# An attention and expert layer: another front, zeros on TensorE, and down weights and rotation table in other pieces

## The chip, the cores and the metric

One Trainium2 chip, one core of it, with its engines TensorE (PE; PEld is its weight load), VectorE (DVE), ScalarE (ACT), GpSimd (POOL) and SyncE (SP, here only an issuer of DMAs). Times are device microseconds of one execution of the whole program. All data are fp32 in DRAM.

## The reference

```python
x = hidden                                # [2048, 256], one batch
xn = layernorm(x)                         # no gain, eps 1e-5
q, k, v = xn @ W.T + b, 16 heads of 16    # q and k rotated (RoPE, even and odd channels)
scores = q k^T / 4; columns 205..1535 masked out   # 205 first and 512 last keys stay
attn = softmax(scores) @ v @ Wo.T + bo
expert = argmax(xn @ router_w.T)          # 8 experts, top 1 with top-2 softmax weight
ffn = weight * (silu(xn gate_w^T) * (xn up_w^T)) @ down_w^T    # inner width 176
out = x + attn + ffn
```

## The kernel before

The kernel is written engine by engine, each with its own program order; semaphores join them. There is no planner: the order around the change is written out by hand, and an engine that waits holds everything behind it on that engine.

**Front.** The 2048 tokens are 16 tiles of 128, in four groups g of four tiles, and eight pairs of two. SP loads x (the first two tiles, the other two of group 0, then groups 1 to 3; between groups 1 and 2 the constants `const`: identity, triangle, ones and some rows, and the router weights `rt`), then `wqk` (k and q weights in one DMA, lines 324 and 325 with the biases `bqk` on the same semaphore), `wv`, the broadcast biases `bvo` and the rotation table `tab` in one DMA of 2 MB (cosine and sine, 2048 columns each). Per group DVE makes statistics (`moments`, lines 903 to 908: four `bn_stats`, four `bn_aggr`, one addition of EPS), ACT the square root (`root`, 1293), DVE the reciprocal and the shift (913, 915), and DVE and ACT normalise two tiles each (919 and 1305; DVE all four in group 3). DVE does `moments(g)` before `normalize(g - 1)`. PE turns the tiles pair by pair (`turn_pair`, 570: four transposes of 128x128 into a PSUM bank), ACT copies a pair to `xnT` (1298), DVE the last pair (942).

**PE's order in the front** (lines 599 to 644): pairs 0 and 1; `project(0)` (594: keys of the first 205 tokens, two halves of 128 channels, two matmuls each); pairs 2 and 3; the router's logits of token block b=0 (576: each block b writes its own 32 rows of one bank); pairs 4 to 7; one of six chunks of v (583); the logits of blocks 1 to 3; one more v chunk; four transposes of the logits (624); two v chunks; the ranks (629 to 632); `project(1)`; two v chunks; 16 matmuls that sum tokens into slots (641), one for each of DVE's 16 lane tiles (1040); `project(2)` and `project(3)`. DVE meanwhile rotates `project(0)`, chooses experts and gives every token a row in an order sorted by expert (977 to 1062), writes the gather indices `token_of`, and then adds bv to the six v chunks into `v_all` (1092). POOL first fills rows of `k_op` and all of `v_all` with ones (481, 489), then waits for `token_of` and gathers the tiles of sorted rows (496), 23 of them. SP stores xn to DRAM group by group (341) for these gathers, loads gate/up weights (342, 2.8 MB), stores the first key part, and loads the down weights `dn` (344 and 345: rows 0 to 79 and 80 to 87 of 88, each row 16 KB; an expert's 176 inner rows are two halves of 88), waits for gather 1 and loads `wo`.

**Expert rows.** 23 steps: PE turns the gathered rows (653), gate and up (667), the hidden rows turned (692, twice 88 columns), down (680, twice 88 rows), and from step 7 maxima of the scores of heads 0 and 1 ahead of time (705), which DVE reduces (1116). The remaining projections and rotations are spread over the steps.

**Heads.** 16 heads of score matmuls (818), exponentials on ACT (1420), probabilities times v (789) and the next heads' maxima (716, 729; DVE 1122, 1125). POOL adds bo to the residual x tile by tile during the heads.

## Time and profile before

| | us |
|---|---|
| median of 3 runs (lowest, highest) | 379.26 (378.15, 379.45) |
| profiled execution, its own time | 379.26 |
| its span in the profile | 377.4 |
| PE busy | 360.1 |
| DVE busy | 331.2 |
| ACT busy | 265.4 |
| POOL busy | 70.1 |

The span is the time between the first and the last instruction seen by the profiler; 1.9 us lie around it. Matmuls are pipelined and their ends modelled, so the sums of PE overlap a little. A timeline row merges neighbouring instructions of one line: start, length, engine, line, operation, tiles, count, and in brackets how long the engine was idle before and what released it.

### The profile page before, as it was taken

To read this page: it belongs to the slowest core of one execution; us is meant where nothing else is said; L and a number is where in the kernel's file an instruction comes from. 1 tells how busy PE (TensorE), PEld (TensorE's weight loads), DVE (VectorE), ACT (ScalarE), POOL (GpSimd) and SP (SyncE) were. 2 spreads that over 40 slices of the span, in tenths; PEclk is the share of its full clock that TensorE was granted. 3 is DMA by queue.
4 is the path that set the end of the run, shared out by engine and by line. 5 is a ranking of instruction groups with operands and counts; after the bars stand their busy time and mean duration, and the time that the engine had idled before them with its cause. 6 is when DMAs were issued, how large, how long until landed. Compare 5 with 4: busy or idle time off the path is not lost.

```text
span 377.4 us, 12257 instructions
## 1 busy us (share of the span) xinstructions
PE 360.1 (95%) x4670; PEld 204.1 (54%) x4670; DVE 331.2 (88%) x684; ACT 265.4 (70%) x538; POOL 70.1 (19%) x87
## 2 busy tenths in 40 slices
PE   0899999999999999999999999999999999999994
PEld 0665566776664564555556546555455554543373
DVE  5869789998768999999999999999999999998464
ACT  1634577664446888888888888888888888899900
POOL 5002845333000021020220202123112021010020
PEclk9999999999999999999999999999999999999999
DMA  7999656756410212223132231322313212111116
GB/s 230 407 396 251 144 156 188 233 159 187 118 64 31 61 33 60 72 64 75 31 88 68 56 75 32 95 80 48 88 40 91 61 49 74 34 46 32 32 32 221
DMA packets 30795, 40.59 MB, mean 108 GB/s; under 512 B 10772, under 2 KB 25876, under 8 KB 30160
## 3 DMA queue, kind: packets, MB, share of 16 engines
q1 hardware_dynamic: 28680, 34.62, 30.9%
q0 software_dynamic: 1872, 5.11, 5.7%
q8 instruction: 38, 0.62, 0.7%
q10 hardware_dynamic: 192, 0.13, 0.1%
q14 instruction: 13, 0.11, 0.1%
HBM read 25.78 MB, written 11.70 MB: 99 GB/s over the span
## 4 chain that ended last, share of the span: by engine, by line
PE 92%; DMA 2%; ACT 2%; SPq 1%; DVE 1%; issue 1%; ACTq 0%; DVEq 0%
PE ps L789 22%; PE ps L818 21%; PE ps L716 14%; PE ps L667 7%; PE ps L729 6%; PE ps L594 5%; PE ps L680 5%; PE ps L797 3%; DMA bqk<-bqk_in 2%; PE ps L705 2%; PE ps L583 1%; PE ps L653 1%; PE ps L692 1%; PE ps L576 1%; PE ps L570 1%
## 5 line engine op out<-in xcount | busy, mean ns | idle before, releaser
L1122 DVE TENSOR_REDUCE mx<-ps 128x1 f32<-128x512 f32 x232 | 150.2, 683 | 4.3 <-PE ps L716 1.5
L1420 ACT ACTIVATE probs<-ps 128x512 f32<-128x512 f32 x192 | 101.9, 598 | 18.3 <-PE ps L818 17.3
L818 PE MATMUL ps<-q_op,k_op 98*32 98x512 bf16 (+1 forms) x1104 | 112.2, 381 | 0.1
L716 PE MATMUL ps<-k_op,q_op 96*32 96x512 bf16 x672 | 76.0, 381 | 0.0
L1125 DVE TENSOR_REDUCE mx_tail<-ps 128x2 f32<-128x410 f32 x116 | 66.8, 576 | 3.2 <-PE ps L729 3.1
L818 PEld LDWEIGHTS ps<-q_op,k_op 98*32 98x32 bf16 (+1 forms) x1104 | 39.6, 96 | 33.6 <-issue 5.6
L789 PE MATMUL ps<-probs,v_op 128*32 128x512 f32 x384 | 52.5, 592 | 0.0
L502 POOL COPY v_op<-v_all 128x192 f32<-128x192 f32 x16 | 7.0, 444 | 187.5 <-PE ps L789 187.5
L1420 ACT ACTIVATE dn<-ps 77x512 f32<-77x512 f32 x64 | 34.3, 592 | 8.2 <-PE ps L818 8.2
L496 POOL DMA_INDIRECT o_st<-sorted_rows,token_of x23 | 26.3, 1143 | 58.1 <-PE ps L653 28.5
L716 PEld LDWEIGHTS ps<-k_op,q_op 96*32 96x32 bf16 x672 | 25.1, 96 | 21.6 <-DVE mx L1122 9.0
L1420 ACT ACTIVATE gu<-ps 128x512 f32<-128x512 f32 x64 | 33.2, 604 | 5.0 <-PE ps L818 5.0
L818 PE MATMUL ps<-parts 98*32 98x512 bf16 (+1 forms) x368 | 36.3, 381 | 0.1
L729 PE MATMUL ps<-k_op,q_op 96*32 96x205 bf16 x672 | 35.7, 251 | 0.0
L729 PEld LDWEIGHTS ps<-k_op,q_op 96*32 96x32 bf16 x672 | 22.1, 97 | 23.1 <-issue 9.4
L1420 ACT ACTIVATE wqk<-ps 128x512 f32<-128x512 f32 x64 | 33.1, 608 | 0.1
L667 PE MATMUL ps<-gu,probs 128*128 x92 | 31.0, 459 | 0.0
L716 PE MATMUL ps<-parts 96*32 96x512 bf16 x256 | 28.4, 380 | 0.0
L1116 DVE TENSOR_REDUCE mx<-ps 128x1 f32<-128x717 f32 x24 | 21.7, 903 | 6.8 <-PE ps L705 6.1
L594 PE MATMUL ps<-xnT,wqk 128*128 128x512 f32 (+1 forms) x48 | 21.1, 584 | 0.2 <-DMA bqk<-bqk_in 0.2
L818 PEld LDWEIGHTS ps<-parts 98*32 98x32 bf16 (+1 forms) x368 | 12.7, 95 | 15.0 <-ACT probs L1420 4.5
L789 PE MATMUL ps<-dn,v_op 77*32 77x512 f32 x128 | 18.8, 592 | 0.0
(142 smaller groups left out, 489.3 us busy)
## 6 DMA issues: line engine op xcount, KB each, us to landing
q_parts<-parts SPq DMA_DIRECT2D x12, 256.0 KB, 2.8
sorted_results<-ys SPq DMA_DIRECT2D x23, 128.0 KB, 2.1
gu<-gu_in SPq DMA_DIRECT2D x1, 2816.0 KB, 14.2
q_op<-q_parts SPq DMA_DIRECT2D x11, 192.0 KB, 3.5
tab<-tab_in SPq DMA_DIRECT2D x1, 2048.0 KB, 11.5
sorted_rows<-xn SPq DMA_DIRECT2D x4, 512.0 KB, 6.3
xnT<-o_st SPq DMA_DIRECT2D x62, 32.0 KB, 2.3
tab<-softmax_recips SPq DMA_DIRECT2D x15, 128.0 KB
```

The source lines that it names most:

```text
L496: pool.indirect_dma_start(out=xs[t % XR], out_offset=None, in_=xn_dram, in_offset=bass.IndirectOffsetOnAxis(ap=token_of[:, t:t + 1], axis= ...
L594: ins = pe.matmul(proj_bank(u, odd), wqk[:, is_q, HID * m + P * odd:HID * m + P * odd + P], xnT[:, m, t0:t0 + n], start=m == 0, stop=m == ...
L667: ins = pe.matmul(bank(b)[:, 0:2 * I], xsT[b][:, P * m:P * m + P], gu[:, bass.ds(e * (HC * 2 * I) + 2 * I * m, 2 * I)], start=m == 0, stop ...
L680: ins = pe.matmul(bank(4 + b)[:, 0:HID], hidT[b][:, P * m:P * m + P], dn[:, bass.ds(e * (2 * HID) + HID * m, HID)], start=m == 0, stop=m == 1)
L716: ins = pe.matmul(bank(t % 2)[r:r + CW, :], q_op[slot][0:KR, P * t + r:P * t + r + CW], k_op[slot][0:KR, 0:NWIDE], start=True, stop=True)
L729: ins = pe.matmul(bank(2)[r:r + CW, NTAIL * n:NTAIL * n + NTAIL], q_op[slot][0:KR, P * t + r:P * t + r + CW], k_op[slot][0:KR, NWIDE:NK], ...
L789: ins = pe.matmul(bank(7)[VW * b:VW * b + VW, :], v_op[slot][0:rows, VW * c:VW * c + VW], prob[c][0:rows, QB * b:QB * b + QB], start=c == ...
L818: ins = pe.matmul(bank(4 + u % RING)[r:r + w, :], k_op[h % OPS][:, c0 + r:c0 + r + w], q_op[h % OPS][:, QB * b:QB * b + QB], start=True, s ...
L1116: dve.tensor_reduce(mx[:, h, t:t + 1], ps[:, EARLY_MAX:EARLY_MAX + NK], AX.X, ALU.max).then_inc(max_reduced, 1)
L1122: dve.tensor_reduce(mx[:, slot, t:t + 1], bank(t % 2)[:, 0:NWIDE], AX.X, ALU.max).then_inc(wide_reduced, 1)
L1125: dve.tensor_reduce(mx_tail[:, slot, 2 * pair:2 * pair + 2], bank(2)[:, 0:2 * NTAIL].rearrange("p (t n) -> p t n", t=2), AX.X, ALU.max).th ...
L1420: act.activation(prob[c][0:rows, QB * b:QB * b + QB], bank(4 + u % RING)[0:rows, :], ACT.Exp, scale=SCALE).then_inc(exp_done, 1)
```

## The change

- **x and constants.** The four groups of x are loaded without anything between them. The identity comes alone, on ACT's queue, as ACT's first instruction; triangle, ones and the rest come later on SP. Key weights, `bqk`, `rt`, `wv`, then the constants, the bias bo (broadcast) and bv as two columns, table part 0 and the query weights follow, each with a semaphore of its own.
- **Statistics.** `normalize(g)` follows `moments(g)` directly, with two of group 3's statistics in front of `normalize(2)`. EPS is the bias of ACT's square root, and the addition on DVE is gone. ACT normalises two tiles of group 3 as well and copies the last pair; DVE copies pair 6.
- **Zeros.** DVE clears 512 columns of `q_op[1]` first, and PE multiplies them into a bank that nothing reads yet: 16 times at the start, then 6, 2, 2 and 2 times between its groups of transposes.
- **PE's order.** Pairs 0 and 1, 2 and 3, `project(0)`, pairs 4 and 5, two v chunks, pairs 6 and 7, all four logits blocks side by side, a v chunk, the transposes of the logits, two v chunks, ranks, `project(1)`, the last v chunk, half of `project(2)`, the slot sums, the other half.
- **v bias.** v is copied without bias by ACT (six copies in place of DVE's six additions). Since the probabilities of a row sum to one, bv times Wo is added to bo: PE makes it with two matmuls ahead of head 0 (from `wo` and the bv columns), DVE adds it to the broadcast bo.
- **POOL.** `v_all` is filled first, the rows of `k_op` only after the logits.
- **Down weights.** The 176 rows of an expert are split as 128 and 48, not as 88 and 88. Three DMAs bring them in pieces of 1 KB: 88 rows, 40 rows (partitions 88 to 127) and 48 rows. They stand behind gate/up and table part 1 and no longer wait for the first key part.
- **Table.** Four DMAs of 512 columns: part 0 in the front, part 1 (last columns) behind gate/up, part 2 behind the down weights, part 3 behind gather 5.

```diff
-        dn = sb("dn", [IH, E * 2 * HID])
+        dn = sb("dn", [P, E * 2 * HID])
...
+        TAB_PARTS = ((0, QB), (S - QB, S), (QB, 2 * QB), (2 * QB, S - QB))
+        TAB_OF = (0, 1, 0, 2, 3, 1)
+        HID_ROWS = ((0, P), (P, I - P))
...
-                if g == 1:
-                    sp.dma_start(const[:], const_d).then_inc(const_in, 16)
-                    sp.dma_start(rt[:], rt_d).then_inc(rt_in, 16)
-            sp.dma_start(wqk[:, 0:2, :].rearrange("p w n -> p (w n)"), wqk_d).then_inc(wqk_in, 16)
-            sp.dma_start(bqk[:], bqk_d).then_inc(wqk_in, 16)
+            sp.dma_start(wqk[:, 0, :], wqk_d[:, 0:HC * HID]).then_inc(wk_in, 16)
+            sp.dma_start(bqk[:], bqk_d).then_inc(bqk_in, 16)
+            sp.dma_start(rt[:], rt_d).then_inc(rt_in, 16)
             sp.dma_start(wv[:], wv_d).then_inc(wv_in, 16)
-            sp.dma_start(bvo[:], bvo_d.broadcast_to([P, 2 * HID])).then_inc(wv_in, 16)
-            sp.dma_start(tab[:].rearrange("p a n -> p (a n)"), tab_d).then_inc(tab_in, 16)
+            sp.dma_start(const[:, C_TRI:C_END], const_d[:, C_TRI:C_END]).then_inc(const_in, 16)
+            sp.dma_start(bias, bvo_d[:, HID:2 * HID].broadcast_to([P, HID])).then_inc(bvo_in, 16)
+            sp.dma_start(bv_col, bvo_d[:, 0:HID].rearrange("a (m p) -> (a p) m", p=P), allow_slow_non_contiguous=True).then_inc(bvo_in, 16)
+            def load_tab(n):
+                c0, c1 = TAB_PARTS[n]
+                sp.dma_start(tab[:, :, c0:c1], tab_d.rearrange("p (a n) -> p a n", a=2)[:, :, c0:c1]
+                             ).then_inc(tab_in[n], 16)
+            load_tab(0)
+            sp.dma_start(wqk[:, 1, :], wqk_d[:, HC * HID:2 * HC * HID]).then_inc(wq_in, 16)
...
-                if g < 3:
-                    sp.wait_ge(xn_on_act, g + 1)
+                sp.wait_ge(xn_on_act, g + 1)
                 sp.dma_start(nv[:, 4 * g:4 * g + 4, :], xn[:, 4 * g:4 * g + 4, :]).then_inc(xn_stored, 16)
             sp.dma_start(gu[:], gu_d).then_inc(gate_up_in, 16)
-            store_part(0, 0)
-            sp.dma_start(dn[0:80, :], dn_d[0:80, :]).then_inc(down_in, 16)
-            sp.dma_start(dn[80:IH, :], dn_d[80:IH, :]).then_inc(down_in, 16)
-            sp.wait_ge(xs_in[1], 16)
+            load_tab(1)
+            by_half = [ap.rearrange("p (e m n) -> p e m n", e=E, m=2) for ap in (dn[:], dn_d)]
+            for m, p0, from_half, h0, h1 in ((0, 0, 0, 0, IH), (0, IH, 1, 0, P - IH), (1, 0, 1, P - IH, IH)):
+                sp.dma_start(by_half[0][p0:p0 + h1 - h0, :, m, :], by_half[1][h0:h1, :, from_half, :]
+                             ).then_inc(down_in, 16)
+            load_tab(2)
+            for u, part in ((0, 0), (0, 1), (0, 2), (1, 0)):
+                store_part(u, part)
+            sp.wait_ge(xs_in[1], 32)
+            load_tab(3)
             sp.dma_start(wo[:], wo_d).then_inc(wo_in, 16)
...
-            for n in range(RING):
-                pool.memset(k_op[n][KR:KM, :], 1.0).then_inc(ones_ready, 1)
-                pool.wait_ge(ones_ready, n + 1)
+            pool.memset(v_all[:], 1.0).then_inc(ones_ready, 1)
+            pool.wait_ge(ones_ready, 1)
...
-            pool.memset(v_all[:], 1.0).then_inc(ones_ready, 1)
-            pool.wait_ge(ones_ready, RING + 1)
+            pool.wait_ge(logits_T_ready, 1)
+            for n in range(RING):
+                pool.memset(k_op[n][KR:KM, :], 1.0).then_inc(ones_ready, 1)
+                pool.wait_ge(ones_ready, n + 2)
...
-            pe.wait_ge(const_in, 16)
-            for pair in range(NT // 2):
+            def keep_running(times):
+                for _ in range(times):
+                    pe.matmul(bank(6), q_op[1][:, 0:P], q_op[1][:, 0:QB], start=True, stop=True)
+            pe.wait_ge(warm_ready, 1)
+            keep_running(16)
+            pe.wait_ge(ident_in, 16)
+            for pair in (0, 1):
                 turn_pair(pair)
-                if pair == 1:
-                    pe.wait_ge(wqk_in, 32)
-                    pe.wait_ge(xnT_ready, 1)
-                    project(0)
-                if pair == 3:
-                    pe.wait_ge(rt_in, 16)
-                    pe.wait_ge(xnT_ready, 2)
-                    for m in range(HC):
-                        logits_part(0, m)
-            pe.wait_ge(wv_in, 32)
-            project_v(V_ORDER[0])
-            for b in range(1, NQB):
-                pe.wait_ge(xnT_ready, min(2 * b + 2, NT // 2 - 1))
+            keep_running(6)
+            for pair in (2, 3):
+                turn_pair(pair)
+            keep_running(2)
+            pe.wait_ge(wk_in, 16)
+            pe.wait_ge(xnT_ready, 1)
+            project(0)
+            keep_running(2)
+            for pair in (4, 5):
+                turn_pair(pair)
+            pe.wait_ge(wv_in, 16)
+            for c in V_ORDER[0:2]:
+                project_v(c)
+            for pair in (6, 7):
+                turn_pair(pair)
+            keep_running(2)
+            pe.wait_ge(rt_in, 16)
+            pe.wait_ge(xnT_ready, NT // 2 - 1)
             pe.wait_ge(last_xnT_ready, 1)
             for m in range(HC):
-                for b in range(1, NQB):
+                for b in range(NQB):
                     ins = logits_part(b, m)
             ins.then_inc(logits_T_ready, 1)
-            project_v(V_ORDER[1])
+            project_v(V_ORDER[2])
             pe.wait_ge(logits_T_copied, 1)
             pe.wait_ge(proj_read, 2)
             for j in range(QB // P):
                 ins = pe.transpose(bank(7)[:, P * j:P * j + P], logits_T[:, P * j:P * j + P], ident)
             ins.then_inc(logits_ready, 1)
-            for c in V_ORDER[2:4]:
+            for c in V_ORDER[3:5]:
                 project_v(c)
             pe.wait_ge(hot_ready, 1)
             pe.matmul(bank(1)[:, 0:NT * E], before_me, hot[:], start=True, stop=False)
                       skip_group_check=True).then_inc(rank_ready, 1)
             pe.wait_ge(logits_read, 1)
             project(1)
-            for c in V_ORDER[4:]:
-                project_v(c)
+            project_v(V_ORDER[5])
+            pe.wait_ge(wq_in, 16)
+            project(2, (0,))
             pe.wait_ge(slot_ready, 1)
             for t in range(NT):
                 pe.wait_ge(lane_ready, t + 1)
                 ins = pe.matmul(slot_sums, at_lane[:, t, :], token_in_slot[:, t, :],
                                 start=t == 0, stop=t == NT - 1)
             ins.then_inc(slots_summed, 1)
-            for u in (2, 3):
-                project(u)
+            project(2, (1,))
+            project(3)
...
+                    rows = HID_ROWS[m][1]
+                    ins = pe.matmul(bank(4 + b)[:, 0:HID], hidT[b][0:rows, P * m:P * m + P],
+                                    dn[0:rows, bass.ds(e * (2 * HID) + HID * m, HID)],
...
+                    i0, rows = HID_ROWS[m]
+                    ins = pe.transpose(bank(3)[0:rows, P * m:P * m + P], hid[b][:, i0:i0 + rows], ident)
...
+            pe.wait_ge(wo_in, 16)
+            pe.wait_ge(bvo_in, 32)
+            for m in range(HC):
+                ins = pe.matmul(bank(3)[:, 0:HID], bv_col[:, m:m + 1].broadcast_to([P, P]),
+                                wo[:, HID * m:HID * m + HID], start=m == 0, stop=m == HC - 1)
+            ins.then_inc(bias_in_psum, 1)
...
-            def moments(g):
-                for t in range(4 * g, 4 * g + 4):
+            def statistics(first, last):
+                for t in range(first, last):
                     if t == 0:
                         dve.wait_ge(x_first, 16)
                     elif t == 2 or t % 4 == 0:
-                        dve.wait_ge(x_in[g], 16)
+                        dve.wait_ge(x_in[t // 4], 16)
                     step(dve.bn_stats(stats[:, t, :], x_sb[:, t, :]))
+            def moments(g):
                 settle()
                 for t in range(4 * g, 4 * g + 4):
-                    step(dve.bn_aggr(mv[:, t, :], stats[:, t, :]))
-                settle()
-                dve.tensor_scalar(var[:, 4 * g:4 * g + 4], mv[:, 4 * g:4 * g + 4, 1], EPS, None,
-                                  ALU.add).then_inc(var_ready, 1)
+                    dve.bn_aggr(mv[:, t, :], stats[:, t, :]).then_inc(var_ready, 1)
             def normalize(g):
                 dve.wait_ge(std_ready, g + 1)
                 dve.scalar_tensor_tensor(shift[:, 4 * g:4 * g + 4], mv[:, 4 * g:4 * g + 4, 0], -1.0,
                                          rstd[:, 4 * g:4 * g + 4], ALU.mult, ALU.mult).then_inc(scale_ready, 1)
-                for t in range(4 * g, 4 * g + (2 if g < 3 else 4)):
+                for t in range(4 * g, 4 * g + 2):
                     ins = dve.tensor_scalar(xn[:, t, :], x_sb[:, t, :], mv[:, t, 0:1], rstd[:, t:t + 1],
                                             ALU.subtract, ALU.mult)
                 ins.then_inc(xn_ready, 1)
+            dve.memset(q_op[1][:, 0:QB], 0.0).then_inc(warm_ready, 1)
+            step(dve.memset(eps[:], EPS))
             step(dve.memset(tiles_upto[:], 0.0))
             step(dve.memset(mx_tail[:], -3.0e38))
+            statistics(0, 4)
             moments(0)
-            for g in range(1, 4):
-                moments(g)
-                normalize(g - 1)
+            normalize(0)
+            statistics(4, 8)
+            moments(1)
+            normalize(1)
+            statistics(8, 12)
+            moments(2)
+            statistics(12, 14)
+            normalize(2)
+            statistics(14, 16)
+            moments(3)
             normalize(3)
             dve.wait_ge(const_in, 16)
-            dve.tensor_copy(id16[:], ident).then_inc(id16_ready, 1)
             step(dve.tensor_tensor(before_me, tri, ones, ALU.subtract))
             step(dve.tensor_scalar(later[:].rearrange("p (e t) -> p e t", e=E),
                                    const[:, C_CNT:C_CNT + NT].rearrange("p (a t) -> p a t", a=1
                                                                         ).broadcast_to([P, E, NT]),
                                    0.0, None, ALU.is_gt))
+            dve.wait_ge(xT_in_psum, NT // 2 - 1)
+            dve.tensor_copy(xnT[:, :, S - 4 * P:S - 2 * P], bank(2).rearrange("p (m n) -> p m n", m=HC)
+                            ).then_inc(last_xnT_ready, 1)
             step(dve.tensor_scalar(same_token[:].rearrange("p (t e) -> p t e", t=NT),
                                    const[:, C_REV:C_REV + E].rearrange("p (a e) -> p a e", a=1
                                                                        ).broadcast_to([P, NT, E]),
                                    float(E), None, ALU.is_lt))
-            dve.wait_ge(xT_in_psum, NT // 2)
-            dve.tensor_copy(xnT[:, :, S - 2 * P:S], bank(3).rearrange("p (m n) -> p m n", m=HC)
-                            ).then_inc(last_xnT_ready, 1)
+            dve.wait_ge(ident_in, 16)
+            dve.tensor_copy(id16[:], ident).then_inc(id16_ready, 1)
...
+                dve.wait_ge(tab_in[TAB_OF[u]], 16)
...
-            v_view = v_all[:].rearrange("p (h c w) -> p h c w", h=HEADS, c=NCH)
-            def add_bv(n):
-                c = V_ORDER[n]
-                rows = CHUNKS[c][1]
-                dve.wait_ge(v_in_psum, n // 2 * 2 + 2)
-                dve.tensor_tensor(v_view[0:rows, :, c, 0:DH], v_bank(c).rearrange("p (h d) -> p h d", h=HEADS),
-                                  bvo[0:rows, 0:HID].rearrange("p (h d) -> p h d", h=HEADS),
-                                  ALU.add).then_inc(v_read, 1)
             route()
             slot_of_tokens()
             second_best()
             copy_token_of()
             experts()
-            dve.wait_ge(ones_ready, RING + 1)
-            dve.wait_ge(wv_in, 32)
-            for n in range(NCH):
-                add_bv(n)
...
+            dve.wait_ge(bias_in_psum, 1)
+            dve.wait_ge(bvo_in, 32)
+            dve.tensor_tensor(bias, bank(3)[:, 0:HID], bias, ALU.add).then_inc(bias_ready, 1)
...
-                act.wait_ge(var_ready, g + 1)
-                act.activation(std[:, 4 * g:4 * g + 4], var[:, 4 * g:4 * g + 4], ACT.Sqrt
-                               ).then_inc(std_ready, 1)
+                act.wait_ge(var_ready, 4 * (g + 1))
+                act.activation(std[:, 4 * g:4 * g + 4], mv[:, 4 * g:4 * g + 4, 1], ACT.Sqrt, bias=eps[:, 0:1],
+                               scale=1.0).then_inc(std_ready, 1)
...
+            act.dma_start(const[:, 0:C_TRI], const_d[:, 0:C_TRI]).then_inc(ident_in, 16)
             root(0)
-            for g in range(1, 4):
-                root(g)
-                normalize(g - 1)
-                copy_xT(2 * g - 2)
-                copy_xT(2 * g - 1)
-            copy_xT(6)
-            act.wait_ge(wqk_in, 32)
-            for odd in range(2):
-                biased(0, odd)
+            normalize(0)
+            copy_xT(0)
+            copy_xT(1)
+            root(1)
+            normalize(1)
+            copy_xT(2)
+            copy_xT(3)
+            root(2)
+            act.wait_ge(bqk_in, 16)
+            biased(0, 0)
+            normalize(2)
+            copy_xT(4)
+            root(3)
+            copy_xT(5)
+            normalize(3)
+            biased(0, 1)
+            copy_xT(7)
+            v_view = v_all[:].rearrange("p (h c w) -> p h c w", h=HEADS, c=NCH)
+            def copy_v(n):
+                c = V_ORDER[n]
+                rows = CHUNKS[c][1]
+                act.wait_ge(v_in_psum, n // 2 * 2 + 2)
+                act.copy(v_view[0:rows, :, c, 0:DH], v_bank(c).rearrange("p (h d) -> p h d", h=HEADS)
+                         ).then_inc(v_read, 1)
+            act.wait_ge(ones_ready, 1)
+            for n in (0, 1):
+                copy_v(n)
...
             highest(0)
+            for n in (2, 3):
+                copy_v(n)
             for odd in range(2):
                 biased(1, odd)
+            for n in (4, 5):
+                copy_v(n)
+            biased(2, 0)
             act.wait_ge(gap_ready, 1)
             act.activation(tk["ratio"][:], tk["gap"][:], ACT.Exp).then_inc(ratio_ready, 1)
-            for odd in range(2):
-                biased(2, odd)
+            biased(2, 1)
+            biased(3, 0)
             middle(0)
-            for odd in range(2):
-                biased(3, odd)
+            biased(3, 1)
```

## Rows read from the trace of the kernel before

**Rows 1.** The profile's page: span, PE, DMA rate in slices of 9.4 us.
```profile
span 377.4 us, 12257 instructions
...
PE 360.1 (95%) x4670; PEld 204.1 (54%) x4670; DVE 331.2 (88%) x684; ACT 265.4 (70%) x538; POOL 70.1 (19%) x87
...
GB/s 230 407 396 251 144 156 188 233 159 187 118 64 31 61 33 60 72 64 75 31 88 68 56 75 32 95 80 48 88 40 91 61 49 74 34 46 32 32 32 221
```

**Rows 2.** Chain of waits in order of time: start us, us, what.
```profile
4.98 7.37 DMA bqk<-bqk_in
...
19.85 0.86 PE ps L583 x4
...
83.79 0.91 DVE mx L1116
...
120.89 0.22 PE ps L716 x4
```

**Rows 3.** Timeline of PE: start us, us, engine, line, what.
```profile
10.30 1.94 PE L570 MATMUL ps<-const,xn 128*128 128x128 f32 x8 [10.30 <-DVE xn L919]
12.39 2.86 PE L594 MATMUL ps<-xnT,wqk 128*128 128x205 f32 x8 [0.15 <-DMA bqk<-bqk_in]
15.09 1.04 PE L570 MATMUL ps<-const,xn 128*128 128x128 f32 x8
...
20.73 1.92 PE L576 MATMUL ps<-xnT,rt 128*32 128x512 f32 x12
...
31.85 1.52 PE L641 MATMUL ps<-v_op,wqk 128*128 128x23 f16 x16
...
40.33 0.44 PE L653 MATMUL ps<-const,o_st 128*128 128x128 f32 x2
```

**Rows 4.** Timeline of DVE, the first 37 us.
```profile
3.74 1.41 DVE L903 BATCH_NORM_STATS2 stats<-x_sb 128x6 f32<-128x256 f32 x4 [2.79 <-DMA x_sb<-x_in]
5.18 0.38 DVE L906 BATCH_NORM_AGGREGATE mv<-stats 128x2 f32<-128x6 f32 x4
5.60 0.97 DVE L908 TENSOR_SCALAR var<-mv 128x4 f32<-128x4 f32 x1
7.21 1.41 DVE L903 BATCH_NORM_STATS2 stats<-x_sb 128x6 f32<-128x256 f32 x4 [0.64 <-DMA x_sb<-x_in]
...
9.14 0.17 DVE L913 RECIPROCAL rstd<-std 128x4 f32<-128x4 f32 x1
...
9.42 0.73 DVE L919 TENSOR_SCALAR xn<-x_sb,mv,rstd 128x256 f32<-128x256 f32 x2
...
30.44 2.68 DVE L1040 TENSOR_SCALAR wqk<-o_st,row_lane_f 128x128 f16<-128x128 f16 x16
...
34.36 2.08 DVE L1092 TENSOR_TENSOR v_all<-ps,bvo 128x256 f32<-128x256 f32 x6
```

**Rows 5.** Timeline of ACT, the first 12 us.
```profile
6.60 0.20 ACT L1293 ACTIVATE std<-var 128x4 f32<-128x4 f32 x1 [4.57 <-DVE var L908]
...
9.54 1.09 ACT L1305 ACTIVATE xn<-x_sb,shift,rstd 128x256 f32<-128x256 f32 x2
11.42 0.59 ACT L1298 COPY xnT<-ps 128x512 f32<-128x512 f32 x1 [0.79 <-PE ps L570]
```

**Rows 6.** Timeline of POOL.
```profile
3.88 2.66 POOL L489 MEMSET v_all<- 128x3072 f32 x1
34.51 1.15 POOL L496 DMA_INDIRECT o_st<-sorted_rows,token_of  x1 [27.96 <-DVE token_of L1051]
```

**Rows 7.** Line 496, the gathers issued at 34.5 and at 39.2: time to landing.
```profile
DMA to landing us min/median/max: 5.8/5.8/5.8
...
DMA to landing us min/median/max: 2.8/2.8/2.8
```

**Rows 8.** Busy us by engine in two stretches; last PEclk, DMA share, GB/s.
```profile
6.00:8.00 2.00, 0.00 (x0) 0.00 (x0) 1.36 (x4) 0.20 (x1) 0.54 (x1) 1.00 0.99 284
...
38.00:40.00 2.00, 2.00 (x6) 0.76 (x4) 1.97 (x4) 0.74 (x2) 1.70 (x2) 1.00 0.44 117
```

33 lines of the change are left out of this document (18 added, 15 removed).

## Prediction

> **What bounds the kernel now.** I read the page first: PE is busy 95% of the span [rows 1]. Then the chain of waits in order of time [rows 2]: until 12.35 it is the loads on SP's queue, ending with the q/k bias that project(0) waits for; from there it is PE with hardly a break up to the heads, where one stop of 2.6 us comes from DVE's early maxima at 83.8. So a microsecond saved ahead of the expert rows is a microsecond of the span, unless something else is then late. PE's timeline [rows 3] shows that the front has two defects. The first transpose starts at 10.30, and the first instructions run at half pace: eight transposes take 1.94 us at 10.30 and eight take 1.04 at 15.09. The granted clock reads 1.00 in every stretch, so the level is read from the pace: 1.2 GHz up to about 14.9, 2.4 GHz after it, and PE had done nothing before 10.30. From 20.73 (three of the four logits blocks) to 40.33 (first transpose of gathered rows) PE works through, 19.60 us.
>
> I compare at two points: L, the start of the last logits matmuls (20.73), and X, the first transpose of gathered rows (40.33). After X the order of PE, DVE and ACT is unchanged but for the bias matmuls.
>
> **DVE and ACT up to L.** DVE now finishes group 0 before it touches group 1 [rows 4]. Statistics 3.74 to 5.15, aggregation 0.38, to 5.56. The separate addition of EPS goes (bias of ACT's root instead). Its first instance took 0.97 us and ended at 6.57; the memset of v_all on POOL ended at 6.54 [rows 4, 6]. It is four columns wide, like the root, which takes 0.20 [rows 5]. The memset now runs first on POOL, so about 0.74 to 3.4, before x is there, and the operation is gone: I count nothing for either. Should something still stretch group 0 by the same 0.80, L moves by 0.45, since group 1 has to wait for its load anyway.
>
> The Trainium skill, "SBUF — State Buffer", section "Who interferes with whom", says that a DVE tensor_scalar in a two-port mode waits for a GpSimd instruction that holds the shared pair. The trace agrees with the rule: the two ends lie 0.03 apart. By the rule the 0.80 goes because the memset has moved; without it, it would go only with the operation, or come back at the next one.
>
> Root 0.20 [rows 5] and its two hand-offs take 0.3: 5.86. Reciprocal to last normalised tile was 9.14 to 10.15, 1.01 [rows 4]: xn group 0 at 6.87, pair 0 on PE at 7.0 instead of 10.30. Group 1: its load was waited for until 7.21 and stays third on SP, so 7.2 + 1.41 + 0.41 + 0.3 + 1.01 = 10.35. Group 2: 1.41 + 0.41, then two statistics of group 3 (0.70) that hide the root, then 1.01: 13.9. Group 3: 0.70 + 0.41 + 0.3 + 1.01 = 16.35; ACT's half of it starts 0.36 after the reciprocal and takes 1.09 [rows 5]: 16.85.
>
> **PE up to L.** The 16 filler matmuls start behind a DVE memset, at about 1.3. Four 512-column bf16 matmuls side by side take 0.22 at the upper level [rows 2], so one takes about 0.22, and 0.44 at the lower: 16 cost 3.5 to 7.0 us, over at 6.5 if the level rises as long after the first work as it did before (10.30 to 14.9), and at 8.3 if it doesn't. I take 6.5, hidden in PE's idle time before 7.0; at the other end they cost pair 0 1.3 us, of which some 0.7 gets to L because ACT's root(1) stands behind copy_xT(0) and (1). Fillers 6, 2, 2 and 2 (1.3, 0.4, 0.4, 0.4) lie in PE's waits for groups 1, 2 and for the last copy; without those waits they would cost 2.6. Pairs 0 and 1 to 8.0, pairs 2 and 3 to 11.5 (0.49 each at the upper pace), fillers to 12.0. Key weights: 2.75 MB had landed at 12.35 [rows 2], 2.3 MB are now ahead of or in wk, at the same rate 10.9 to 11.2. project(0) at the upper pace is half its 2.86 [rows 3], 1.4: 13.4. Pairs 4 and 5 wait for group 2: 13.95 to 15.0. V chunks 0 and 1, at 0.86 [rows 2]: 16.7. Pairs 6 and 7 to 17.7, ACT's copy 0.59 [rows 5] with hand-offs: L = 18.5; 18.6 with slack. That is 2.1 us earlier. Bounds: 18.1 (pair 7 right behind ACT's half at 16.85, then the copy, is 18.0) to 20.1 (the 0.45 and 0.7 above and some slack of hand-offs).
>
> **L to X.** Before, the b=0 block of the logits ran alone ahead of L; now four run side by side in the 1.92 of three. V chunk 1 moves ahead of L: 0.86 less. 19.60 - 0.86 = 18.74, so X = 37.3, 3.0 earlier. The slot sums keep pace with DVE's sixteen lanes, which ended at 33.12 [rows 4], PE's at 33.37 [rows 3]; half of project(2) now stands ahead of them, so they run from 30.7 to 32.2 (native 1.52) and DVE's lanes end by 31.0. DVE loses six bias additions (2.08 us, [rows 4]) and ACT gets six copies, at most 0.59 each [rows 5], where it waits for PE's projections; the additions stood ahead of rotations that were needed 2 us later, so this is worth nothing on the chain.
>
> **Gathers.** Gather 0 was issued at 34.51 and landed 5.8 later, 40.31 [rows 6, 7], just when PE was through: no slack before. It follows the slot sums by 1.14: 33.3 now, 1.2 earlier, not 3.0. Gather 3, issued with less before it, needed 2.8 [rows 7]; between 38 and 40 the DMA share was still 0.44 at 117 GB/s [rows 8], the tail of the down weights. So gather 0 lands between 36.1 and 39.1. Bytes: some 9.3 MB now stand ahead of the down weights, against 10.5; the slices of the page [rows 1] make 2.17 MB by 9.4 us, 6.0 by 18.9 and then 396 GB/s, so they are through at 27.2 instead of 30.2. The 1.44 MB of down weights fell into the slice of 251 GB/s, 5.7 us, and I keep that for the 1 KB pieces (x, also in 1 KB pieces, ran at 284 GB/s [rows 8], 5.1 us): 32.9; table part 2 (0.52 MB) 34.2. The queue is nearly empty as gather 0 starts, so it lands at about 37, and I take X = 37.4. For the 1 KB pieces below nothing is not excluded, above it is the 39.1.
>
> The Trainium skill, "DMA: Bandwidth & Descriptors", section "Why a DMA increments its semaphore by 16 and not by 1", says that a DMA uses the largest number of engines up to 16 that divides its slowest dimension. By it 88 and 40 rows use 11 and 10 engines; the busiest gets 64 + 32 + 24 = 120 pieces where an even spread has 88, 7.0 us in place of 5.1 at the 284 GB/s of rows 8: table part 2 ends at about 35.5. No row shows the engines one by one. It does not push gather 0 beyond 37.4 by itself, but it is what would make the rival of the gathers true.
>
> Down weights and table have cover: down is first used two expert rows after X, part 1 (ahead of down in the queue) by unit 1's rotation at about 33, parts 2 and 3 behind X. SP's wait is now for gather 5, not gather 1; behind it stand table part 3, wo and two stores of unit 1, wanted after that.
>
> **Bias on PE.** Two fp32 matmuls of 256 columns, the same as a V chunk: 0.86 [rows 2], between the last down and head 0, where PE is the chain. At most 0.1 of it covers the wait for ACT's last ys. DVE's addition (0.35) falls in its wait for the first maxima. Lower end 0, upper end 1.2 (both on the chain). I take +0.85.
>
> **Sum.** -2.9 at X, +0.85 behind: -2.05. The profiled execution took 379.26 with a span of 377.4, which is also the median of the runs: 379.26 - 2.05 = 377.2.
>
> **Rivals.** (a) Gathers bind: landing 39.1, X moves 1.2 only, 378.9. For it: no slack before [rows 3, 7]; against: the lighter queue. (b) PE's low level stays or comes back: it idles 1.1 us between pairs 1 and 2. If the zeros don't hold the level, then from pair 2 at 10.5 pairs 2 and 3 take 1.9, four fillers 1.8, project(0) 2.9, pairs 4 to 7 3.9, the two V chunks 3.5 and the copy 0.7: L = 25.2, 4.5 late; less 0.86 and plus 0.85, 383.7, slower than before (and the logits would take longer too). It decides from L = 20.7 on; at the upper level there are 2.1 us to spare. For it: PE was at the lower level for its first 4.6 us; against: the hole is short and filled on both sides. (c) The bias is hidden and L is at its lower bound, 2.6 + 0.86 earlier: 379.26 - 3.5 = 375.8, if gather 0 lands by 36.9; the waits around head 0's start speak for it a little, but PE's own stream has no hole there. (d) The fillers don't do what they are there for: the upper level comes at 14.9 as before. project(0) then ends at 14.9, pairs 4 and 5 at 15.8, V at 17.5, pairs 6 and 7 at 18.5, L = 19.3 and the time 377.9.
>
> **Chances.** Forecast 0.52 (376.4 to 378.1), gathers 0.18, (d) 0.08, (c) 0.12, (b) and like delays 0.10. Half a per cent, about what a measurement tells from no change, is 1.9 us: faster means below 377.4. The forecast lies on that border: of its 0.52 some 0.36 are below it, and (c)'s 0.12 with some small parts of (a) and (d), 0.52 in all. Slower (above 381.2) 0.06, the worse part of (b); the rest, 0.42, is no change. Range 375.6 to 379.3.
>
> **What would show it.** First xn transpose at 7.0 and pairs 2 and 3 within 0.1 of 1.0 us together (level); var row gone and no DVE row stretched before 7; L at 18.6; X at 37.4 with PE, not a DMA, as its releaser; bias matmuls 0.86 ahead of head 0; from there on everything earlier by 2.05. Wrong if L is later than 19.5, X is released by gather 0, or the gap changes between X and head 0, above all at the stop of 83.8.

## The result, and the profile after

The changed kernel takes 387.64 us, median of 4 runs (386.29 to 388.60), against 378.81 for the one before in the same comparison: ratio 1.0225, interval 1.0198 to 1.0252. It is 8.8 us slower; 377.2 was forecast, and the range ended at 379.3. The profiled execution took 388.58 with a span of 386.8, 9.4 longer than [rows 1]. Times below are medians of all executions, while the ratios leave out those that were in a slower state, over 1.5% above the kernel's fastest (one of a_88_tab2, two of a_96_split_bias, five of a_96_sb_front).

The page of the changed kernel (span, PE, then PEclk and GB/s in slices of 9.7 us):

```profile
span 386.8 us, 12335 instructions
PE 374.1 (97%) x4702; PEld 204.2 (53%) x4702; DVE 328.3 (85%) x675; ACT 269.8 (70%) x546; POOL 67.9 (18%) x87
PEclk9999699999999999999999999999999999999999
GB/s 234 328 364 187 181 178 181 211 152 165 145 90 57 15 57 49 62 69 47 74 77 56 58 53 87 64 58 73 80 65 73 33 94 64 47 22 41 31 39 222
```

PE is busier by 14 us and yet later: some of its work is zeros, some runs at half pace, and its expert steps are longer. The slice from 38.7 to 48.4 has a granted clock below full. Its timeline answers [rows 3]:

```profile
1.20 6.52 PE L625 MATMUL ps<-q_op 98*128 98x512 bf16 x16 [1.20 <-DVE q_op L966]
7.55 1.04 PE L593 MATMUL ps<-const,xn 128*128 128x128 f32 x8
8.43 1.46 PE L625 MATMUL ps<-q_op 98*128 98x512 bf16 x6
11.75 1.14 PE L593 MATMUL ps<-const,xn 128*128 128x128 f32 x8 [1.86 <-DVE xn L962]
...
19.63 1.92 PE L599 MATMUL ps<-xnT,rt 128*32 128x512 f32 x16 [0.29 <-ACT xnT L1340]
...
31.65 0.68 PE L677 MATMUL ps<-v_op,wqk 128*128 128x23 f16 x16
...
43.10 0.69 PE L689 MATMUL ps<-const,o_st 128*128 128x128 f32 x2 [5.52 <-DMA o_st<-sorted_rows,token_of]
43.58 3.62 PE L617 MATMUL ps<-xnT,wqk 128*128 128x512 f32 x4
...
57.32 1.00 PE L717 MATMUL ps<-dn,probs 128*128 x3
...
124.37 1.32 PE L717 MATMUL ps<-dn,probs 128*128 x4 [0.24 <-ACT probs L1422]
125.62 1.13 PE L896 MATMUL ps<-wo,bvo 128*128 128x256 f32 x4
126.68 0.61 PE L754 MATMUL ps<-k_op,q_op 96*32 96x512 bf16 x8
```

Before, the first down, the last down and head 0 stood here:

```profile
52.13 0.81 PE L680 MATMUL ps<-dn,probs 88*128 x3
...
114.33 1.13 PE L680 MATMUL ps<-dn,probs 88*128 x4 [0.29 <-ACT probs L1358]
115.38 0.62 PE L716 MATMUL ps<-k_op,q_op 96*32 96x512 bf16 x8
```

Read as differences between the two kernels, point by point: L 1.10 earlier (19.63 for 20.73); X 2.77 later (43.10 for 40.33); first down 5.19 later, of which 2.42 came between X and it; last down 10.04 later, 4.85 more; head 0 at 126.68 for 115.38, 11.30 later, and of the last 1.26 the bias is 1.06. The last stretch gives 1.9 back (the span ends 2.2 after DVE's last additions, 4.1 before). So 2.8 + 2.4 + 4.9 + 1.3 - 1.9 = 9.4, with rounding.

The wait in front of X, in the chain of waits (start, us, what) and in a table of stretches with the columns of [rows 8]:

```profile
33.45 9.60 DMA o_st<-sorted_rows,token_of
43.06 0.04 issue
43.10 0.69 PE ps L689 x2
43.79 3.41 PE ps L617 x4
```

```profile
20.00:30.00 10.00, 10.00 (x51) 6.09 (x44) 7.45 (x28) 3.11 (x7) 2.08 (x3) 1.00 1.01 359
...
38.00:40.00 2.00, 0.00 (x0) 0.00 (x0) 2.00 (x3) 0.30 (x1) 1.40 (x2) 1.00 1.03 196
40.00:42.00 2.00, 0.00 (x0) 0.00 (x0) 0.01 (x1) 0.00 (x0) 0.00 (x0) 0.81 0.81 200
42.00:44.00 2.00, 0.90 (x3) 0.82 (x4) 0.00 (x0) 0.18 (x1) 0.00 (x0) 0.50 0.70 231
```

Gather 0 was issued 1.06 us earlier than in [rows 6] and took 9.6 to land where it took 5.8 [rows 7], with the DMA share at 1.03 up to 40 instead of 0.44 [rows 8]. PE idled from 37.6 to 43.1, its granted clock fell to 0.50 (1.2 GHz of 2.4; this is the "level" below), and the half projection behind X took 3.41 instead of 1.72.

### The profile page after: what moved, and what is told of

Same layout as the page of the kernel before. It is cut to its first block, busy times and chain, and to the rows that moved or that the text cites. A ratio compares the mean times of both kernels' runs of the same rounds, so it can differ in the third digit from the quotient of the medians.

```text
span 386.8 us, 12335 instructions
## 1 busy us (share of the span) xinstructions
PE 374.1 (97%) x4702; PEld 204.2 (53%) x4702; DVE 328.3 (85%) x675; ACT 269.8 (70%) x546; POOL 67.9 (18%) x87
## 4 chain that ended last, share of the span: by engine, by line
PE 89%; DMA 4%; DVE 3%; ACT 2%; issue 1%; SPq 0%; POOLq 0%; ACTq 0%; DVEq 0%
PE ps L827 21%; PE ps L856 21%; PE ps L754 14%; PE ps L703 7%; PE ps L717 6%; PE ps L767 6%; PE ps L835 3%; PE ps L617 3%; DMA o_st<-sorted_rows,token_of 2%; PE ps L743 2%; DMA x_sb<-x_in 2%; PE ps L730 2%; PE ps L689 1%; PE ps L606 1%; PE ps L593 1%
## 5 line engine op out<-in xcount | busy, mean ns | idle before, releaser
L518 POOL DMA_INDIRECT o_st<-sorted_rows,token_of x23 | 24.1, 1048 | 51.1 <-PE ps L689 40.5
L703 PEld LDWEIGHTS ps<-gu,probs 128*128 128x128 f32 x92 | 16.0, 193 | 5.6 <-issue 0.7
```

What stands on the lines that cost most here:

```text
L518: pool.indirect_dma_start(out=xs[t % XR], out_offset=None, in_=xn_dram, in_offset=bass.IndirectOffsetOnAxis(ap=token_of[:, t:t + 1], axis= ...
L703: ins = pe.matmul(bank(b)[:, 0:2 * I], xsT[b][:, P * m:P * m + P], gu[:, bass.ds(e * (HC * 2 * I) + 2 * I * m, 2 * I)], start=m == 0, stop ...
```

## Experiments

"After" is the changed kernel; each edit is made to it unless said otherwise. Each was timed beside the kernel before, whose median was between 378.8 and 379.5; ratios are to that kernel. L, X, the landing of gather 0 and the start of head 0 come from one profiled execution of each kernel, which is not always near the median (a_88_1k's took 379.46, a_96_sb_front's 377.51).

| kernel | us (runs) | ratio (interval) | L | X | gather 0, us to land | head 0 |
|---|---|---|---|---|---|---|
| after | 387.64 (4) | 1.0225 (1.0198, 1.0252) | 19.63 | 43.10 | 9.6 | 126.68 |
| a_88_rows | 381.83 (10) | 1.0072 (1.0047, 1.0097) | 18.31 | 40.80 | 8.6 | 119.28 |
| a_88_1k | 381.42 (8) | 1.0063 (1.0035, 1.0091) | 18.29 | 40.26 | 8.1 | 117.69 |
| a_128_big | 385.20 (4) | 1.0174 (1.0128, 1.0220) | 19.20 | 39.90 | 6.8 | 122.76 |
| b_128_big | 383.33 (4) | 1.0122 (1.0077, 1.0168) | 21.05 | 40.50 | | 120.55 |
| a_88_late | 383.46 (4) | 1.0106 (1.0056, 1.0156) | 19.00 | 36.78 | 3.2 | 121.86 |
| a_128_late | 389.21 (5) | 1.0258 (1.0231, 1.0285) | 18.59 | 36.37 | 3.2 | 124.20 |
| a_88_late_nofill | 385.75 (4) | 1.0170 (1.0141, 1.0198) | 20.14 | 37.92 | 3.2 | 122.86 |
| a_88_1k_keep | 379.69 (10) | 1.0022 (0.9996, 1.0049) | 18.79 | 41.07 | 8.4 | 117.02 |
| a_96_tab2 | 381.85 (8) | 1.0066 (1.0033, 1.0100) | 18.92 | 39.48 | 6.7 | 117.16 |
| a_88_tab2 | 378.85 (10) | 0.9978 (0.9953, 1.0003) | 18.71 | 39.66 | 7.1 | 115.62 |
| a_128_tab2 | 386.53 (4) | 1.0167 (1.0123, 1.0212) | 18.54 | 40.25 | 7.8 | 124.24 |
| b_112_big | 383.76 (4) | 1.0112 (1.0066, 1.0157) | 20.93 | 40.73 | 6.0 | 120.79 |
| a_96_split | 381.41 (11) | 1.0040 (1.0014, 1.0066) | 18.74 | 36.94 | about 4 | 118.99 |
| a_96_split_bias | 380.73 (12) | 1.0027 (0.9999, 1.0055) | 19.15 | 36.93 | | 117.93 |
| a_96_sb_front | 380.22 (12) | 0.9999 (0.9959, 1.0039) | 18.29 | 36.07 | | 114.12 |

### Shape of the expert's halves, and the pieces of its weights

**a_88_rows**: the halves and the pieces of before, in the new place.

```diff
-        HID_ROWS = ((0, P), (P, I - P))
+        HID_ROWS = ((0, IH), (IH, IH))
...
-            for m, p0, from_half, h0, h1 in ((0, 0, 0, 0, IH), (0, IH, 1, 0, P - IH), (1, 0, 1, P - IH, IH)):
...
+            sp.dma_start(dn[0:80, :], dn_d[0:80, :]).then_inc(down_in, 16)
+            sp.dma_start(dn[80:IH, :], dn_d[80:IH, :]).then_inc(down_in, 16)
```

> The changed kernel with the down weights split 88 and 88 again and loaded as 80 and 8 rows of 16 KB, at the new place in the queue. My theory has two causes, and this run undoes both. Shape: each expert row of PE costs 0.3 us more with 128 and 48 rows (3.10 against 2.80); it must go back to 2.80. DMA: the 1 KB pieces fill the queue, gather 0 lands after 9.6 us, X is at 43.1 and PE falls to its lower level; here gather 0 lands after 3 to 6 us and X is at 38 to 40. Time 377.5 to 379.5. Rival 1, only the shape matters and the late gather comes from the rest of the new order (table parts, early stores): X stays near 43, time about 382.5. Rival 2, the bias and the front cost it: step and X go back but the time stays above 383.

**a_88_1k**: halves of 88, each loaded in pieces of 1 KB (two DMAs).

```diff
+            for m in range(2):
+                sp.dma_start(by_half[0][:, :, m, :], by_half[1][:, :, m, :]).then_inc(down_in, 16)
```

> As the run with 88 and 88 rows of 16 KB, but loaded in 1 KB pieces, two DMAs of 88 rows each. If the pieces are what fills the queue, X is again near 43 with the lower level behind it, and the time is the changed kernel's less the shape, 387.6 - 5.0 = 382.5. If it was the cutting into 40 rows on partitions 88 to 127 (the DMA that held SP for 7.2 us) and not the pieces, gather 0 lands by 6 us after its issue and the time is 378 to 379.5.

**a_128_big**: 128 and 48, the weights laid out in DRAM so that a partition's half is one piece of 8 KB.

```diff
+            for m, rows in ((0, P), (1, I - P)):
+                sp.dma_start(dn[0:rows, m * E * HID:(m + 1) * E * HID],
+                             dn_d[0:rows, m * E * HID:(m + 1) * E * HID]).then_inc(down_in, 16)
```

> The changed kernel with its 128 and 48 rows kept, but laid out in DRAM so that two DMAs bring 128 rows and 48 rows in pieces of 8 KB. Shape theory: the step stays at 3.10. DMA theory: gather 0 lands early (3 to 5 us), X at 38 to 39 and no fall of the level: 387.6 - 4.5 - 2.2 = 381. If the pieces are not the cause of the late gather, X stays at 43 and the time at 387.6.

**b_128_big**: the kernel before with 128 and 48 in 8 KB pieces, and nothing else.

```diff
-            sp.dma_start(dn[0:80, :], dn_d[0:80, :]).then_inc(down_in, 16)
-            sp.dma_start(dn[80:IH, :], dn_d[80:IH, :]).then_inc(down_in, 16)
+            (the two loads of a_128_big)
...
+                    rows = HID_ROWS[m][1]
+                    ins = pe.matmul(bank(4 + b)[:, 0:HID], hidT[b][0:rows, P * m:P * m + P],
```

> The kernel before with 128 and 48 rows alone, in 8 KB pieces at the old place. Shape theory: PE's step grows from 2.80 to 3.10 before step 14 and by some 0.2 after; 23 steps cost 6, less the 2.6 of DVE's stop at 83.8, which the slower PE hides: 379 + 3 to 4.5 = 382 to 383.5. Rival (the step grew in the changed kernel for another reason, such as the late start): no change, 379.

Undoing the shape, and with it the load by three DMAs, takes the ratio from 1.0225 to 1.0063 or 1.0072. Alone in the kernel before, the shape costs 1.0122, 4.6 us (4.3 by the medians), as expected. From the first down to the last, b_128_big takes 67.06 (52.24 to 119.30), against 62.20 before and 67.05 after. The traces of the other kernels fall into the same two groups, unless PE waits for a transfer in between: 62.2 to 62.3 with 88 and 88 or 96 and 80, 67.0 to 67.1 with 128 and 48 or 112 and 64. So the expert rows are the largest single term, and they belong to the shape, not to the front.

The half of the theory that blamed the pieces failed. a_88_rows was expected at 377.5 to 379.5 with gather 0 landing after 3 to 6 us; it took 381.83 and 8.6. a_88_1k met neither of its two cases (382.5, or 378 to 379.5), and its pieces of 1 KB cost nothing beside those of 16 KB. a_128_big was expected at 381 and took 385.20; its two DMAs of 8 KB pieces were better than three of 1 KB pieces by 2.4 us in the medians (1.9 by the ratios, whose intervals overlap a little), and gather 0 landed in 6.8 instead of 9.6.

The stream of weight loads (PEld) shows where a step grows. After (start, us, in brackets the idle time of the load stream):

```profile
83.76 0.30 PEld L717 LDWEIGHTS ps<-dn,hidT 128*128 128x128 f32 x2
84.39 0.29 PEld L717 LDWEIGHTS ps<-dn,hidT 48*128 48x128 f32 x2 [0.33 <-issue]
85.02 0.11 PEld L743 LDWEIGHTS ps<-k_op,q_op 96*128 96x128 bf16 x2 [0.33 <-issue]
```

Before, the same place of a step:

```profile
73.92 0.73 PEld L680 LDWEIGHTS ps<-dn,probs 88*128 88x128 f32 x4
74.68 0.32 PEld L705 LDWEIGHTS ps<-k_op,q_op 96*128 96x128 bf16 x2
```

With two halves of 88 the four loads run on without a break beneath the matmuls. With 128 and 48 the load of the short half, and the load that follows the short half, each come 0.33 later. PE's step from one gate/up group to the next is 3.10 (82.46 to 85.56) for 2.80 (72.62 to 75.42), all of it between the start of down and what follows it: 1.16 for 0.87. Over the 22 steps from the first down to the last that is some 0.34 in the early ones, 0.30 in the middle and 0.22 where two early maxima stand in a step; where ACT's copy of the hidden rows had held PE 0.8 before (at 65.5) the step even shrinks by 0.62, and the step at the 83.8 of [rows 2] doesn't grow. The sum is the 4.85.

The Trainium skill, "TensorE: Matmul & The Clock Gate", section "Step-by-step: what each phase is for", says that PE pulls a weight load ahead of running matmuls where row groups don't conflict or it goes to the background buffer, and that the number of rows doesn't matter for the load's time. The trace agrees on the time (0.29 for two loads of 48 rows, 0.30 for two of 128). Of the pulling ahead it shows only that it went by the row counts of neighbouring loads. No run tells which of the two conditions is behind that.

**b_112_big**: the kernel before with 112 and 64 rows, from b_128_big.

```diff
-        HID_ROWS = ((0, P), (P, I - P))
+        HID_ROWS = ((0, 112), (112, I - 112))
```

> The kernel before with the down rows as 112 and 64, in 8 KB pieces. For 128 and 48 it took 383.3 and PE's weight load stood idle 0.33 us ahead of each 48-row load and of the load behind it. Theory: loads for at most 64 rows and for more can't be lined up ahead of each other, so 64 rows cost as 48 do: 383. Rival, the cost comes with fewer than 64 rows or with three quadrants: no cost, 379.

```profile
75.83 0.30 PEld L683 LDWEIGHTS ps<-dn,probs 112*128 112x128 f32 x2
76.47 0.29 PEld L683 LDWEIGHTS ps<-dn,probs 64*128 64x128 f32 x2 [0.33 <-issue]
77.09 0.11 PEld L709 LDWEIGHTS ps<-k_op,q_op 96*128 96x128 bf16 x2 [0.33 <-issue]
```

1.0112 (383.76, with 383 expected) with the same two holes: 64 rows cost what 48 cost. With 96 and 80 (in a_96_tab2, below) the four loads run through again and the step is 2.80, so it isn't every unequal split that costs:

```profile
74.78 0.73 PEld L718 LDWEIGHTS ps<-dn,probs 96*128 96x128 f32 x4
```

### When the down weights and the table move

**a_88_late** (from a_88_rows): down weights and table part 2 behind gather 1. **a_128_late**: the same move in the changed kernel.

```diff
+            store_part(0, 0)
+            sp.wait_ge(xs_in[1], 16)
             (the down weights)
             load_tab(2)
-            for u, part in ((0, 0), (0, 1), (0, 2), (1, 0)):
+            for u, part in ((0, 1), (0, 2), (1, 0)):
                 store_part(u, part)
```

> The run with 88 and 88 rows of 16 KB, but the down weights and table part 2 (2 MB together) are issued only when gather 1 has landed. The runs so far showed gather 0 landing 6.8 to 9.6 us after its issue whatever the pieces of the down weights, so the theory is now: it is the 2 MB issued ahead of it, not their pieces. It then lands within 4 us of its issue at 32.1, PE is its own bound again at X = 37.0 (L 18.3 + 18.7), the level doesn't fall, and the time is 379.06 - 3.3 + 1.0 (bias) = 376.8, 376.3 to 377.8. Rival 1: the gathers are slow because of the order of key stores or of gate/up weights: X stays at 40, 381. Rival 2: the down weights now come late for step 2 (PE would wait for them at about 48): 379 to 381.

> The changed kernel, with its 128 and 48 rows and its 1 KB pieces, only down weights and table part 2 issued behind gather 1. Queue theory: X at 37 to 38.5, no fall of the level, but the step stays 3.10 and costs the 4.3 us measured alone: 379.06 - 2.8 + 1.1 + 4.3 = 381.5. If the second DMA's seven us on SP come back and hold the key stores, up to 384.

In the front this does what was expected, and shows the front's own worth: with the queue idle (30 to 36: share 0.09, 26 GB/s) gather 0 lands in 3.2 us and X is 36.78 and 36.37, earlier than the 37.4 forecast. The times miss: 383.46 for the 376.3 to 377.8 expected, 389.21 for 381.5 to 384. What X gains is lost from 6 us later on. Waits, stretches and PE's timeline of a_88_late:

```profile
PE ps L689 <- DMA o_st<-sorted_rows,token_of: 6.2, 1, 6.2
```

```profile
30.00:36.00 6.00, 6.00 (x30) 2.82 (x29) 5.50 (x18) 3.76 (x7) 2.87 (x2) 1.00 0.09 26
...
40.00:42.00 2.00, 2.00 (x7) 0.98 (x6) 1.30 (x3) 0.73 (x3) 1.39 (x3) 1.00 1.03 262
```

```profile
42.06 1.35 PE L703 MATMUL ps<-gu,probs 128*128 x4
49.64 0.69 PE L689 MATMUL ps<-const,o_st 128*128 128x128 f32 x2 [6.24 <-DMA o_st<-sorted_rows,token_of]
50.12 3.62 PE L617 MATMUL ps<-xnT,wqk 128*128 128x512 f32 x4
```

The bulk now lies beside gather 3, which was issued at 38.12, took 11.5 us to land and holds PE from 43.4 to 49.64; the level falls there instead (0.50 from 50 to 54). Neither rival of a_88_late had named that gather. In a_128_late PE waits 3.5 for the down weights themselves. The stop follows the bulk.

**a_88_tab2**, **a_128_tab2** (from a_88_rows and after): only table part 2 (0.52 MB) behind gather 1. **a_96_tab2**: the same with 96 and 80 rows in 8 KB pieces.

```diff
             (the down weights, in their new place)
-            load_tab(2)
+            store_part(0, 0)
+            sp.wait_ge(xs_in[1], 16)
+            load_tab(2)
```

> 88 and 88 rows of 16 KB at the new place, table part 2 behind gather 1. Against the first run with 88 rows (381.8, gather 0 after 8.6 us) only 0.5 MB moves from before gather 0 to behind gather 1. If the bytes ahead count, gather 0 lands 1.5 to 3 us earlier, X at 38 to 39, time 378 to 380. If the slow part is the down weights as 80 and 8 rows, X stays at 40 or later, 381.

> The changed kernel with its three DMAs of 1 KB pieces, only table part 2 behind gather 1. SP was held by the second of them for seven us, so its rate is the limit: gather 0 lands 1.5 to 3 us earlier than 43.1 at best, X 40 to 41.5, level falls still in part: 387.3 - 2 = 385.5. If X stays at 43 (387.5) table part 2 has no part in it; if X gets to 38, 382.

> The changed kernel with 96 and 80 rows (two DMAs in 8 KB pieces, at the new place) and only table part 2 (0.5 MB) behind gather 1. The late runs showed that 2 MB issued at once hold back whatever gather comes in the next nine us, and that the queue was empty from 30 to 38. So: down weights in time to be through by 34 to 36, gather 0 lands 4 to 5 us after its issue, X at 37 to 38, no stop at gather 3, level held. Shape: both parts above 64 rows, so the step is 2.80 as with 88. Time 379.3 - 2.3 = 377.0 (376.3 to 378.3). Rival for the shape: any unequal halves cost, then the step is 3.10 and the time 381. Rival for the queue: bulk of any kind ahead of gather 0 holds it, X at 40 and the level falls: 380.5.

a_88_tab2 is the best by its ratio, 0.9978, and its interval reaches 1.0003: not told apart from the kernel before. The 378.85 is in the expected 378 to 380. Gather 0 lands in 7.1 us instead of 8.6, so the bytes ahead count; its X is 39.66. In the profiled execution the clock stayed at 1.00, but not in all: five executions with a mean granted clock of 0.999 or 1.000 took 377.14 to 378.64 us, four with 0.995 took 379.06 to 379.81. First to last down is 62.24, that of before. With 128 and 48 the same move leaves 1.0167 (386.53 for 385.5 expected; X 40.25 is in its 40 to 41.5). 96 and 80 have the short step too, but in their profiled execution gather 0 still took 6.7 us, the level fell (0.50 at 42 to 44), and they stay at 381.85 and 1.0066, where 376.3 to 378.3 was expected.

**a_96_split** (from a_96_tab2): first half of the down weights ahead, second behind gather 1, table part 2 behind gather 3.

```diff
+            (down weights, 96 rows)
+            store_part(0, 0)
+            sp.wait_ge(xs_in[1], 16)
+            (down weights, 80 rows)
+            (store_part (0, 1), (0, 2), (1, 0))
+            sp.wait_ge(xs_in[3], 16)
+            load_tab(2)
```

> 96 and 80 rows in 8 KB pieces. The 96-row half stands at the new place, the 80-row half (0.66 MB) behind gate/up and gather 1, table part 2 behind gather 3. Queue theory: with only 0.79 MB of down weights ahead, the queue is through by 33 and gather 0 lands within 4.5 us of its issue at 32.5, X at 37.0 to 37.5; what is issued later is small enough not to hold gather 3 (wanted at 43.5). Level held. Time 379.2 - 2.2 = 377.0, against 378.9 for 88 rows with table part 2 late. Rival: any bulk next to the gathers costs, whatever its size, then X at 37 but PE stops later for gather 3 or for the down weights, 378 to 380.

```profile
PE ps L746 <- DMA q_op<-q_parts: 2.9, 1, 2.9
```

No gather holds PE for more than 0.3 here, and X is 36.94. The new wait, up to 66.70, is for query rows, whose stores come later on SP's queue: 2.9 us. The level falls around it (0.62 from 64 to 68, 0.52 from 68 to 72). The time is 381.41, 1.0040, where 377.0 was expected; the rival, bulk beside the gathers costs whatever its size, said 378 to 380.

### The zeros, the level, the bias, the constants

**a_88_late_nofill** (from a_88_late): no zeros at all; all five calls go.

```diff
-            keep_running(16)
...
-            keep_running(6)
```

> As the late run with 88 rows, without any of the zeros. If the zeros hold the upper level, transposes 0 to 3 run at 1.9 us for eight, project(0) at 2.8, and L comes 0.7 to 1.5 later than with them (18.3), as most of it hides behind DVE: time +0.7 to +1.5. If they do nothing, L and time stay. If PE's short bursts between waits never reach the upper level, the v chunks and logits too are slow: +4 us.

```profile
7.32 1.94 PE L593 MATMUL ps<-const,xn 128*128 128x128 f32 x8 [7.32 <-DVE xn L957]
11.19 1.97 PE L593 MATMUL ps<-const,xn 128*128 128x128 f32 x8 [1.93 <-DVE xn L957]
12.95 2.71 PE L617 MATMUL ps<-xnT,wqk 128*128 128x205 f32 x8
15.50 1.32 PE L593 MATMUL ps<-const,xn 128*128 128x128 f32 x8
```

PE stays at its lower level up to about 15, and L is 20.14 for 19.00; the time is 385.75 for 383.46. The zeros are worth 1.1 us at L, as expected, and up to 1.8, since group 1 of x was there 0.7 earlier without them (7.15 for 7.87). In the time it is 2.3, more than the 0.7 to 1.5 expected; both kernels have a 6 us stop behind X, four executions each, and intervals that overlap.

**a_88_1k_keep** (from a_88_1k): 18 matmuls of zeros ahead of X, where PE only waits for gather 0.

```diff
             load_expert(0)
+            for _ in range(18):
+                pe.matmul(bank(0), q_op[1][:, 0:P], q_op[1][:, 0:QB], start=True, stop=True)
             turn_rows(0)
```

> The run with 88 rows in 1 KB pieces, with 18 more zero matmuls (3.9 us) in the place where PE waits for gather 0. X stays where it was (40.3). Theory: PE's level fell to 1.2 GHz in that wait, and it made half of project(4) take 2.98 instead of 1.72 and the next pieces longer; with zeros the level holds and the time falls by 1.3 to 2.0 us from 381.4. If the level has no part in it, the time stays at 381.4.

```profile
36.57 4.05 PE L811 MATMUL ps<-q_op 98*128 98x512 bf16 x18
41.07 0.44 PE L688 MATMUL ps<-const,o_st 128*128 128x128 f32 x2 [0.45 <-DMA o_st<-sorted_rows,token_of]
41.34 1.88 PE L616 MATMUL ps<-xnT,wqk 128*128 128x512 f32 x4
```

Without them, in a_88_1k:

```profile
40.26 0.69 PE L688 MATMUL ps<-const,o_st 128*128 128x128 f32 x2 [4.02 <-DMA o_st<-sorted_rows,token_of]
40.74 3.19 PE L616 MATMUL ps<-xnT,wqk 128*128 128x512 f32 x4
```

X itself is 0.8 later in this pair, and the kernel still 1.7 us faster (379.69 for 381.42; 1.3 to 2.0 was expected, and the intervals of the two ratios overlap). The granted clock stays 1.00, and the projection takes 1.88 for 3.19. So the fall of the level was a cost of its own, on top of the wait. The executions say the same: none of the eight without the zeros has a mean clock above 0.996; seven of the ten with them have 0.999 or 1.000 and took 378.69 to 380.66, the other three (0.994 to 0.996) 381.02 to 382.38.

**a_96_split_bias** (from a_96_split): the bias matmuls in step 14, DVE's addition in step 21.

```diff
+        BIAS_AT, BIAS_READ_AT = 14, 21
...
+                if s == BIAS_AT:
+                    (the two bias matmuls, into a bank of the early maxima)
```

> As the run with the halves split over time, with the two bias matmuls moved from the place ahead of head 0 into step 14 of the experts, where PE waits for DVE's maxima (2.6 us at 83.8 before), and DVE's addition moved to step 21. If the bias costs its 1.03 us on the chain where it was and nothing in PE's stop, the time falls by 1.0 against that run. If the stop is not real slack (DVE is the bound there and the score it waits for comes later by 0.86), it falls by less than 0.3.

Head 0 comes 1.06 earlier (117.93 for 118.99); the time moves by 0.7, between the 1.0 and the 0.3 of the two cases and within the scatter of these executions.

**a_96_sb_front** (from a_96_split_bias): constants and router weights between groups 1 and 2 of x again.

```diff
+                if g == 1:
+                    sp.dma_start(const[:, C_TRI:C_END], const_d[:, C_TRI:C_END]).then_inc(const_in, 16)
+                    sp.dma_start(rt[:], rt_d).then_inc(rt_in, 16)
```

> As the run with the bias moved, with triangle/ones and router weights again between x groups 1 and 2, as before. x group 1 landed at 7.1 before and at 7.1 to 8.5 in the changed kernels, with groups 2 and 3 right behind it, and L moved with it (18.3 to 19.6). If what stands behind group 1 slows it, it lands at 7.1 again and L is at 18.3 in the profile, time -0.5; if it only varies from run to run, no change within 0.3.

Group 1 of x was there at 7.15 (8.49 after), L is 18.29 and X 36.07, the earliest of all. So what stands behind group 1 does bear on its landing. PE's wait for query rows is down to 1.8, and the level didn't fall behind it. The twelve executions lie between 374.78 and 382.02, and their median is 1.3 us above that of the kernel before (378.91), though the ratio is 0.9999 (0.9959 to 1.0039): no gain that can be told. Here too the time goes with the mean clock: 374.78 at 1.000 (one execution), 377.51 to 380.29 at 0.994 to 0.997 (six), 380.74 to 382.02 at 0.990 and 0.991 (five). Only one of them has a trace, so where the clock fell in the others isn't known.

## Why the prediction was wrong

**The front, up to L: the mechanism was right, and one load was mis-sized.** First transposes at 7.55 (7.0 said); the sixteen zeros over at about 7.5 (6.5), most of them at the lower pace; pairs 2 and 3 together 1.14, 0.04 beyond the tenth allowed above 1.0; the addition of EPS is gone and no DVE row is stretched much (1.47 for 1.41). L = 19.63 is in the bounds, 1.0 above the 18.6, and just past the 19.5 that the prediction had named as a sign of being wrong. The main reason is one row, which answers [rows 4]:

```profile
8.49 1.41 DVE L947 BATCH_NORM_STATS2 stats<-x_sb 128x6 f32<-128x256 f32 x4 [1.25 <-DMA x_sb<-x_in]
```

The prediction kept group 1's load at 7.2. It landed at 8.47. Where it was there by about 7.1, L was 18.3. From L on, PE ran out of work at 37.58, 17.95 behind L where 18.74 was said. The slot sums took 0.68 and not 1.52: that figure of [rows 3] was the pace of DVE's lanes, and not, as the prediction had it, PE's own. In a_88_late and a_128_late, where gather 0 doesn't bind, X follows L by 17.78.

**The gathers: the step that failed first.** "The queue is nearly empty as gather 0 starts" is what the trace contradicts. The down weights held SP until 29.73 to issue, table part 2 was issued at 29.77, and the DMA share stayed at about 1 until 40:

```profile
20.14 9.59 SPq L361 DMA_DIRECT2D dn<-dn_in  x3
29.77 2.40 SPq L340 DMA_DIRECT2D tab<-tab_in  x1
```

The estimate had the down weights through at 32.9 and the table at 34.2, at rates of [rows 1] (251 GB/s for the down weights). The slice that began at 9.7 moved 328 GB/s for the 407 assumed from before, and 30 to 40 ran under 200 at full share. Rival (a) named the mechanism, X released by gather 0, and had a chance of 0.18, but its upper bound, the 39.1, came from adding 5.8 to the issue at 33.3. A landing time measured beside one load is no upper bound beside a heavier one: 9.6 was found. That a_88_late lands it in 3.2 shows that the bulk is what holds it.

The Trainium skill, "DMA: Bandwidth & Descriptors", section "Why a DMA increments its semaphore by 16 and not by 1", gave 11 and 10 engines for 88 and 40 rows. With table part 2 ahead, down weights of 128 and 48 rows, which split by 16 under that rule, left gather 0 at 6.8; those of 88, 40 and 48 rows at 9.6, of 88 and 88 at 8.1. That fits it; a_88_rows, with 80 of its 88 rows in one DMA, took 8.6, which doesn't. With table part 2 moved away it was 6.7 for 96 and 80 rows, 7.1 for 80 and 8, and 7.8 for 88, 40 and 48. No run shows the engines one by one.

**The level.** Rival (b) had it fall in the front, where the zeros held it. It fell behind X, since a 5.5 us wait was nowhere in the plan: 2.2 us more from X to the first gate/up of the chain (4.53 for 2.37), nearly all of the 2.42. a_88_1k_keep shows that the level was a cost of its own.

**"After X the order of PE, DVE and ACT is unchanged but for the bias matmuls": the step that failed by most.** The order is unchanged, but the shape of two halves is not, and the prediction priced the 128 and 48 rows at nothing without saying so. It is 4.85 us in the trace and 4.6 in b_128_big. No rival held it. Only the last of the prediction's signs, that the gap between X and head 0 would change, points this way, and that gap grew by 8.5 us.

**The bias.** 0.85 said, 1.06 measured to head 0, on the chain as said. Rival (c), in which it was hidden, is out; rival (d) too, since pairs 2 and 3 ran at the upper pace from 11.75.

**The sum.** Forecast -2.9 at X and +0.85; measured +2.8 at X, +2.4 for the level and around it, +4.9 for the shape, +1.3 at head 0, -1.9 at the end. What a_96_split_bias and a_96_sb_front show is that an X three or four us earlier is there to be had (3.4 and 4.3), but most of it is lost among the transfers of the expert rows: in a_96_sb_front, head 0 is 1.3 earlier than before, with the bias already out of the way.

**Open.** Why the bulk slows gathers and stores as much as it does, by engine or by queue; why x's group 1 lands between 7.1 and 8.5 from run to run; why the clock falls in one execution and not in the next of the same kernel, with which much of the scatter of up to 7 us goes; which rule of the weight loads makes some splits cost and others not; and whether there is a place for the 2 MB of down weights and table without a new stop.

## What to carry over

Another split of the rows can change how the weight loads overlap with the matmuls (128 and 48, 112 and 64 did; 96 and 80 didn't): look at the load stream of one step before pricing it at nothing. If the front of a kernel is made faster than its transfers, price the first late gather by the bulk in flight beside it, and add what the clock costs behind the wait. A bulk load moved out of one gather's way stands in the next one's, so judge the move by the whole stage and not by the wait that it removes.

## What the runs showed of the hardware

- Weight loads of 48 and of 64 rows beside ones of 112 or 128 (and the load of 96 rows behind them) came 0.33 us late each, and a step took 3.10 for 2.80; 88 with 88 and 96 with 80 showed no such hole.
- An indirect gather landed in 3.2 us with the DMA share at 0.09 and in 6.7 to 9.6 with the down weights in flight; gather 3 of a_88_late took 11.5.
- Issuing DMAs of 1 KB pieces can hold SP: three of them took it 9.6 us in the changed kernel (20.14 to 29.73, with gate/up weights in flight), while two of 16 KB pieces took 1.0 before (24.44 to 25.46) and 1.1 in a_88_rows (18.83 to 19.94). It isn't the pieces alone: the same three took 2.6 in a_128_late (37.87 to 40.45), where the DMA share had been 0.08 from 30 to 36 and 0.22 up to 38.
- Behind PE's wait of 4.0 us the granted clock was 0.50 (a_88_1k, 40 to 42), and 1.00 again from 44; with zeros in the wait it stayed at 1.00 in the profiled execution (a_88_1k_keep). A wait of 2.6 in a_96_tab2 was followed by 0.50 too, one of 3.0 in a_88_tab2 by 1.00, so the length of the wait alone did not tell.
